# Cross attention with two key sets: the spread matmuls of every unit move behind the weighted-value matmuls

## What is computed

```python
text, ip = encoder_hidden_states[:, :77, :], encoder_hidden_states[:, 77:, :]
q = _split_heads(hidden_states @ Wq.T, H)
out_text = _merge_heads(_attend(q, split(text @ Wk.T), split(text @ Wv.T), sm_scale))
out_ip = _merge_heads(_attend(q, split(ip @ Wk_ip.T), split(ip @ Wv_ip.T), sm_scale))
out = (out_text + out_ip) @ Wo.T + bo
return out + residual
```

## Time and profile before

| | |
|---|---|
| Median of three runs | 714.46 us (714.28 to 715.46) |
| Span of the profiled execution | 712.9 us |
| What lies around the span (median less span) | 1.6 us |
| PE matmuls busy | 679.8 us (95%) |
| PE weight loads busy | 560.9 us (79%) |
| ACT, DVE, POOL busy | 493.3, 441.4, 224.0 us |
| TensorE clock granted over the span | 0.988 of full speed |

### The profile page before, as it was taken

How to read it: one execution, slowest core, us unless ns; L and a number is a source line. 1 busy time by engine, 2 the same in 40 slices (tenths; PEclk the granted TensorE clock), 3 DMA queues, 4 the chain that set the end, 5 groups by cost and what they waited for, 6 DMA issues and landing times.

```text
span 712.9 us, 18904 instructions
## 1 busy us (share of the span) xinstructions
PE 679.8 (95%) x6514; PEld 560.9 (79%) x6514; DVE 441.4 (62%) x956; ACT 493.3 (69%) x1078; POOL 224.0 (31%) x261
## 2 busy tenths in 40 slices
PE   8959789999999999999999999999999999999997
PEld 8958566777877788778877887888778877887777
DVE  5786667665757565665656565655657575756633
ACT  3984687876767676767776777677767776776641
POOL 4020103243423324242424233242434233242333
PEclk9989899999999999999999999999999999999999
DMA  8940021313131312222121312112131313111211
GB/s 321 408 191 16 17 62 33 83 48 94 51 91 46 92 50 77 58 56 86 52 82 52 90 52 82 52 56 86 46 95 47 89 46 95 51 51 47 61 47 66
DMA packets 34690, 57.44 MB, mean 81 GB/s; under 512 B 4832, under 2 KB 27232, under 8 KB 34400
## 3 DMA queue, kind: packets, MB, share of 16 engines
q1 hardware_dynamic: 34656, 56.99, 26.0%
HBM read 35.34 MB, written 10.49 MB: 64 GB/s over the span
## 4 chain that ended last, share of the span: by engine, by line
PE 53%; ACT 30%; issue 10%; DVE 6%; ACTq 1%; POOL 0%; DVEq 0%
PE pv_ps L780 11%; ACT q_stack L397 9%; PE q_ps L711 9%; ACT probs L405 8%; PE x_ps L711 7%; PE b_ps L752 7%; PE a_ps L735 7%; PE x_ps L789 5%; PE sum_ps L769 5%; ACT y L428 3%; ACT q_hi L390 3%; ACT pv_sb L410 2%; ACT attn_hi L434 1%; DVE k_stack L631 1%; DVE k_stack L641 1%
## 5 line engine op out<-in xcount | busy, mean ns | idle before, releaser
L405 ACT ACTIVATE probs<-b_ps 77x512 f32<-77x512 f32 x320 | 181.1, 591 | 153.3 <-PE b_ps L752 151.7
L571 DVE TENSOR_REDUCE row_max<-a_ps 128x4 f32<-128x308 f32 x320 | 138.5, 474 | 86.6 <-PE a_ps L735 84.0
L562 DVE TENSOR_TENSOR q_stack<-q_ps,q_hi 32x256 fp32r<-32x256 f32 x320 | 134.3, 420 | 36.0 <-ACT q_hi L390 32.3
L397 ACT ACTIVATE q_stack<-q_hi 32x256 fp32r<-32x256 f32 x320 | 133.0, 416 | 10.0
L352 POOL TENSOR_TENSOR attn_lo<-scaled,attn_hi 128x256 fp32r<-128x256 f32 x80 | 58.9, 737 | 182.3 <-ACT attn_hi L434 182.3
L752 PE MATMUL b_ps<-q_stack,k_stack 98*77 98x256 f32 x640 | 115.6, 282 | 0.6 <-ACT probs L405 0.5
L735 PE MATMUL a_ps<-k_diag,q_hi 128*128 128x308 f32 x320 | 93.7, 333 | 7.5 <-DVE row_max L571 7.5
L598 DVE TENSOR_TENSOR scaled<-x_ps,pv_sb 128x512 f32<-128x512 f32 x75 | 51.9, 692 | 68.2 <-PE x_ps L789 67.6
L358 POOL TENSOR_TENSOR res<-y,res 128x256 f32<-128x256 f32 x70 | 51.1, 730 | 136.7 <-ACT y L428 136.7
L347 POOL TENSOR_TENSOR scaled<-scaled 128x256 f32<-128x256 f32 x80 | 58.5, 732 | 102.6 <-DVE scaled L598 102.5
L752 PEld LDWEIGHTS b_ps<-q_stack,k_stack 98*77 98x77 f32 x640 | 85.7, 147 | 2.3 <-ACT probs L405 1.3
(11 more groups left out here) (111 smaller groups left out, 939.3 us busy)
## 6 DMA issues: line engine op xcount, KB each, us to landing
x_raw<-x_in SPq DMA_DIRECT2D x16, 640.0 KB, 4.1
q_stack<-q_stack SPq DMA_DIRECT2D x80, 128.0 KB, 2.3
res<-x_in SPq DMA_DIRECT2D x75, 128.0 KB, 2.1
y_out<-res SPq DMA_DIRECT2D x75, 128.0 KB, 1.7
stage<-wk_in SPq DMA_DIRECT2D x6, 640.0 KB, 8.2
stage<-wv_in SPq DMA_DIRECT2D x6, 640.0 KB, 10.3
wq_raw<-wq_in SPq DMA_DIRECT2D x1, 1600.0 KB, 9.3
wo_raw<-wo_in SPq DMA_DIRECT2D x1, 1600.0 KB, 14.7
```

The lines of the kernel that those rows point to most:

```text
L397: done = nc.scalar.activation(q_stack[0:D, u.slot, j, :], q_hi[j * D:(j + 1) * D, u.slot, :].bitcast(F32), ACT.Copy)
L405: nc.scalar.activation(probs[0:KEYS, j, :], b_ps[j % 2][0:KEYS, :], ACT.Exp).then_inc(b_drained, 1)
L562: done = nc.vector.tensor_tensor(q_stack[D:2 * D, u.slot, j, :], q_ps[rows, 0:N], q_hi[rows, u.slot, :].bitcast(F32), ALU.subtract)
L571: nc.vector.tensor_reduce(row_max[:, u.slot, br, :, sub], bank[:, 0:BLK].rearrange("p (j n) -> p j n", j=GROUP), AXIS.X, ALU.max).then_inc ...
```

## The change

The condition on g goes. `spread_inverse` stands behind `weigh_values` in every unit.

```diff
                 row_sums(u)
-                if norm.exists() and norm.g > 0:
-                    spread_inverse(norm)
                 weigh_values(u)
-                if norm.exists() and norm.g == 0:
+                if norm.exists():
                     spread_inverse(norm)
```

## The result

The changed kernel takes 683.88 us (683.04 to 684.4, four runs) against 714.83 us in the four runs of the kernel before beside it: a ratio of 0.957, with a 95% interval of 0.955 to 0.958. The change wins 31 us. I had forecast 24 us, and 687 to 696 us as the range, so the sign and both causes were right and the size of one of them was not.

A forecast was written before the change was run, and what follows sets the result against it. PE was taken to bound the kernel, losing time around narrow-to-full changes and the wait for y. Steady stretch 23.8 plus early units 1.1 minus end 0.6 gave 24.3 us less, 690.2 us; range 687 to 696 us.

The forecast's parts named there:

- both causes: Between row sums and next scores: the spread no longer waits for y, and one narrow-to-full change with about 0.4 us idle goes.
- What bounds the kernel: PE bounds; its weight loads idle before the spread and before first scores; row sums to scores falls from 2.66 to 2.20 us.
- The steady stretch: Units 10 to 77: 53 periods fall from 8.00 to the g = 0 period of 7.56 us; 23.8 us with one later stretch.
- my signs of being wrong: Waits for row maxima before L735 or L741 in every unit, or scores to row sums longer than 5.35 us.
- this one term: Earlier row maxima than with g = 0 might save another 0.03 us a unit, 1.6 us more, giving 687.0 us.
- Early units: Units 6 to 9 and unit 78: 0.22 us won in each, 1.1 us in all; bounds 0 and 1.1 us.
- ACT: ACT's wait of 2.31 us before a unit's first exponential falls to 1.9 us, so ACT still waits for PE.
- The end: Behind unit 79 `scaled` begins about 0.86 us later against the row sums; a loss of 0.6 us, between 0 and 0.9.
- only the wait for y goes: Rival, before the spread: only the 5.6 us that matmul rows show as waiting for y is won; 709 us, chance 0.03.
- nothing is won: Rival, row sums to scores: narrow groups don't pack, 2.62 us end to end against 2.66 us; 712 us, chance 0.02.
- the maxima become the bound: Rival, PE's later score pieces: later `scaled` delays DVE's maxima, each unit loses 1.1 and wins 0.44 us; 750 us, chance 0.03.
- A part given back: Rival, every unit: ACT or DVE has less time to catch up, a 0.2 us wait returns; 701 us, chance 0.06.

The follow-up runs named there:

- the early drain in the old order: Kernel before, old order kept, with ACT's copy of the fourth head's rows of q_stack left out in the loop over units: 699.91 us.
- the run with a lighter ACT: Changed kernel with ACT's copy of the fourth head's rows of q_stack left out in the loop over units: 681.65 us.

## Why the prediction was right or wrong

*What bounds the kernel* held. PE was the engine, and the two idle times of its weight loads were the places. Their length is not the price, though: 0.41 us of idle time went with each change, and a pair of changes measured 0.33 us. The stretch from row sums to scores is 2.21 us in every unit, where I said 2.20 us.

*The steady stretch* is the step that failed. I let the period of a unit with g = 0 (7.56 us) stand for the others and wrote that its delay of the row maxima is "what already costs nothing". It cost 0.10 us. What misled me was that the part behind the scores takes 5.35 us in a unit with g = 0 as in all others, so it looked free. It was the sum of two things: 0.10 us won, because the scores follow full matmuls instead of narrow ones, and 0.10 us lost to DVE, which comes from the inverse. Units with g > 0 get the gain without the loss: 5.25 us. I had even worked out that their maxima would come less late, and used it as a comfort against a loss, not as a gain: the bounds allowed 0.03 us a unit for it, and it was 0.10 to 0.11 us. That is 5.8 us of the 6.3 us by which the forecast was off, and it put the result outside the range. All my rivals and all my signs of being wrong looked for a smaller gain; below 688.6 us I had only this one term.

*Early units*: the same term. I took 0.22 us a unit from the stretch before the scores, and the period fell from 6.39 to 6.05 us, 0.34 us: a whole pair of changes. These units wait 0.28 us for ACT's last exponential before and after, so here the gain passes through ACT's chain, which begins with the scores.

*ACT* was right, at 1.72 us of waiting where I said 1.9 us (0.10 us of the difference is the same term), and the run with a lighter ACT shows that it is off the path. *The end*: a loss of 0.4 us where I said 0.6 us. The chunk waits 0.78 us for `scaled` and begins 0.71 us later against the row sums, where I said about 0.86 us. Its last matmul comes 0.62 us later, since its wait for POOL falls from 0.26 to 0.17 us, and 0.2 us more is made up behind it.

*The rivals.* That only the wait for y goes fell with the early drain in the old order: that wait is 11.5 us in the whole stretch, twice what the matmul rows showed for it, and 17.6 us are the order's own. That nothing is won, with the weight loads of the values held back until the sums are through, fell with the rows of unit 43: those loads begin at 388.29, and the sums' records run until 388.68, and with the total. That the maxima become the bound was real as a mechanism, and its price was 0.10 us in one unit of five, well short of the 0.44 us from which it would have decided. A part given back did not happen.

## What to carry to other kernels

On PE count the changes between groups placed side by side on parts of the array and matmuls that take it whole, and set groups of one kind side by side; a group that waits for another engine goes behind both, if nothing waits for it at once. When a part of the kernel already has the new order, it is the best price there is, but compare it piece by piece: an equal total can be a gain and a loss of the part's own that cancel. A delay that was "absorbed" has to be looked for in the spacing of the instructions behind it, since the list of waits left it out here.

## What the runs showed of the hardware

A pair of changes between the groups of 32 columns at four places of the array and the full matmuls costs 0.33 us here, in three settings: the old order against the new with y out of the way (7.78 and 7.45 us a unit), the spread split in two (2.54 and 2.21 us), and the early units (6.39 and 6.05 us, where the gain also passes through ACT). Only 0.22 us of it show in the stretch where the matmuls were moved. The rest shows in the full matmuls that follow the narrow ones, so that an interval which ends at their start misses it. The Trainium skill, "TensorEngine Tiling (Array Packing)", section Key Properties, says that a change of the tiling mode drains TensorE. The trace agrees, with 0.41 us without a weight load at each change to full matmuls, and adds the price.

The number of columns alone does not make such a change. `turn_maxima` (L741) loads 16 columns between full matmuls, once in each unit. In the changed kernel, unit 43:

```profile
392.76 0.28 PE L711 MATMUL q_ps<-x_hi,wq_hi 128*128 128x256 f32 x1
392.88 0.27 PE L741 MATMUL a_ps<-ident,row_max 128*16 128x128 f32 x1
392.90 0.36 PE L711 MATMUL q_ps<-x_hi,wq_lo 128*128 128x256 f32 x1
```

The matmul behind it begins 0.02 us later, and in none of the 80 units do the weight loads behind it wait. So the price goes with the groups placed side by side at several places of the array. Whether it depends on how many places or which, no run here shows.
